# Fused attention and mixture-of-experts layer: how GpSimd issues its row scatters, k copies, bias and weight loads during attention

## What is computed

```python
x = L0_attn_hidden_states                       # 32 x 256 x 128, float32
xn = _layernorm(x)
# layer: pre-norm attention with factored weights, 16 heads of 8, causal, then a gelu MLP with factored weights
Q = einsum(LN(xn), q_U, q_V) + q_b              # K and V alike
attn = softmax(where(causal, Q K^T / sqrt(8), -1e9));  ctx = attn V
h = xn + ctx @ out_U @ out_V + out_b
layer = h + gelu(LN(h) @ fc1_U @ fc1_V + fc1_b) @ fc2_U @ fc2_V + fc2_b
# experts: softmax over 9, the best 2 of each token, silu-gated feed-forward of width 352
out = sum over the 2 chosen e of cw[t, e] * ((silu(xn Wg[e]) * (xn Wu[e])) @ Wd[e])
return x + layer + out
```

## Time and profile before

| | us |
|---|---|
| median of 3 runs | 1068.63 (1065.06 to 1071.98) |
| the profiled execution | 1073.31 |
| its span, first to last instruction | 1071.6 |
| TensorE busy | 997.1 (93%) |
| VectorE busy | 709.6 (66%) |
| ScalarE busy | 559.6 (52%) |
| GpSimd busy | 432.5 (40%) |

### The profile page before, as it was taken

One profiled execution on the slowest core, in us unless ns is written; L12 is line 12 of the kernel. 1 busy time (PEld: TensorE's weight loads), 2 busy tenths in 40 slices (PEclk: granted clock), 3 DMA queues, 4 the chain that ended last, 5 costly groups with the idle time before them and its releaser, 6 DMA issues. The chain is left out here.

```text
span 1071.6 us, 25659 instructions
## 1 busy us (share of the span) xinstructions
PE 997.1 (93%) x7829; PEld 773.1 (72%) x7829; DVE 709.6 (66%) x3240; ACT 559.6 (52%) x1285; POOL 432.5 (40%) x559
## 2 busy tenths in 40 slices
PE   4768999999999999999998895999999999899997
PEld 4535566666666666666655554999999999899996
DVE  5658589777777777777765661555555555457887
ACT  1552355556556556556553473555555555554442
POOL 9462032044544354444345442544544444441010
PEclk9675799999999999999999986999999999999999
DMA  8285276364464464454435213222222222218884
GB/s 228 81 228 170 78 206 180 82 165 120 102 153 112 122 160 121 101 114 109 109 93 113 84 58 103 64 67 61 64 62 64 72 64 60 81 40 254 236 236 129
DMA packets 133560, 127.16 MB, mean 119 GB/s; under 512 B 17274, under 2 KB 113652, under 8 KB 133428
## 3 DMA queue, kind: packets, MB, share of 16 engines
q1 hardware_dynamic: 109860, 67.83, 23.9%
q0 software_dynamic: 20592, 56.43, 19.5%
q10 hardware_dynamic: 2976, 1.26, 0.5%
HBM read 57.15 MB, written 42.60 MB: 93 GB/s over the span
## 5 line engine op out<-in xcount | busy, mean ns | idle before, releaser
L1363 DVE CUSTOM_DVE_ANT_0 att_masked_st<-att_m_ps,att_mask_st 128x128 bf16<-128x128 f32 (+1 forms) x1024 | 312.8, 353 | 122.2 <-PE att_m_ps L969 69.5
L784 ACT ACTIVATE att_probs<-att_t_ps 128x512 f32<-128x512 f32 x384 | 228.9, 598 | 219.6 <-PE att_t_ps L993 203.8
L625 POOL DMA_INDIRECT slot_x<-att_xs,att_slot_now x128 | 128.5, 1004 | 181.0 <-PE att_t_ps L993 130.9
L1616 POOL DMA_INDIRECT y_scratch<-moe_y,moe_row_now x136 | 132.8, 976 | 155.4 <-DVE moe_y L1870 102.8
L1864 DVE TENSOR_TENSOR moe_hidden<-moe_gate,moe_up_ps 128x352 f32<-128x352 f32 x136 | 70.9, 521 | 111.9 <-issue 85.3
L993 PE MATMUL att_t_ps<-att_mask_ts,att_ident_b 128*128 128x256 bf16 (+1 forms) x384 | 126.2, 329 | 0.0
L1693 PE MATMUL moe_y_ps<-w_down,moe_hidden_t 128*128 (+1 forms) x816 | 114.2, 276 | 3.8 <-DVE moe_y L1870 3.8
L1791 ACT ACTIVATE moe_gate<-moe_gate_ps 128x352 f32<-128x352 f32 x136 | 63.1, 464 | 96.8 <-PE moe_up_ps L1676 96.8
L1693 PEld LDWEIGHTS moe_y_ps<-w_down,moe_hidden_t 128*128 128x128 f32 (+1 forms) x816 | 101.8, 191 | 5.7 <-issue 5.5
L589 POOL DMA_DIRECT2D att_k_stack<-att_qk_parts x96 | 54.7, 575 | 89.3 <-PE att_t_ps L993 70.5
L992 PE MATMUL att_t_ps<-even_stack,att_k_stack 97*128 97x512 f32 x192 | 82.6, 430 | 4.1 <-DMA even_stack<-att_neg_max 3.8
(11 more groups left out here) (263 smaller groups left out, 2150.4 us busy)
## 6 DMA issues: line engine op xcount, KB each, us to landing
att_k_stack<-att_qk_parts POOLq DMA_DIRECT2D x96, 128.0 KB
slot_x<-att_xs POOLq DMA_DIRECT2D x17, 516.0 KB, 3.7
moe_x<-slot_x SPq DMA_DIRECT2D x34, 258.0 KB
att_xs<-xn_scratch SPq DMA_DIRECT2D x32, 256.0 KB
mlp_rows<-y_scratch POOLq DMA_DIRECT2D x16, 512.0 KB, 5.4
even_stack<-att_qk_parts SPq DMA_DIRECT2D x192, 32.0 KB
att_odd_stack<-att_qk_parts SPq DMA_DIRECT2D x192, 32.0 KB
xn_scratch<-att_probs POOLq DMA_DIRECT2D x16, 256.0 KB, 3.1
```

The source lines that it names most:

```text
L625: pool.indirect_dma_start(env["slot_x"][:], bass.IndirectOffsetOnAxis(ap=slot_now[c.parity][:, col:col + 1], axis=0), xs[c.parity][:, t, k ...
L784: act.activation(probs[:, m % PT, :], t_ps[m % 2][:], ACT.Exp).then_inc(exp_done, 1)
L1363: last = dve.tensor_tensor_reduce(out=masked_st[m % 2][:, part], in0=m_ps[m % 2][:, part], in1=mask_st[:, SEQ - width:], scale=1.0, scalar ...
L1616: pool.indirect_dma_start(env["y_dram"][:], bass.IndirectOffsetOnAxis(ap=row_now[q.parity][:, t:t + 1], axis=0), y[c.parity][:], None).the ...
```

## The change

GpSimd's step no longer goes by slots but by pairs of score units, 12 in a step. At every pair it waits for the first unit of the pair, and then issues at most one scatter or fill, at most one k part, the bias or one weight load.

- Scatters: 9 per step in steps 3 to 10, 12 per step in steps 11 to 14, and 8 in step 15, counted through over chunks (`ROWS_OF`, `ROWS_AT`).
- Fills: at the first 8 pairs of steps 0 and 1, and the first of step 2.
- k parts: one at each of the pairs 1, 2, 3 for (next chunk, b = 1), and at the pairs 8, 9, 10 for (chunk two ahead, b = 0).
- Bias at pair 7. Weight loads at the pairs 10 and 11 of steps 3 to 10.
- SyncE takes the chunk whose xs it loads from a table `XS_AT` made from the scatters' places, at one of three points of its step: a new one after the first 12 copies of q parts, after `stack_max(p, 1)`, and after `stack_max(next, 0)`.

```diff
-        LATE, PAIRED_FROM = 3, chunks - 3
-        XS_MID = {s: s - LATE + 1 for s in range(LATE - 1, PAIRED_FROM)} | {s: 2 * s - chunks + 1 for s in range(PAIRED_FROM, chunks)}
-        XS_LAST = {s: 2 * s - chunks + 2 for s in range(PAIRED_FROM, chunks - 1)}
+        LATE = 3
+        W_STEPS, LAST_ROWS = 8, 8
+        ROWS_OF = {step: 9 if step < LATE + W_STEPS else 12 for step in range(LATE, chunks - 1)} | {chunks - 1: LAST_ROWS}
+        ROWS_AT = {step: sum(n for k, n in ROWS_OF.items() if k < step) for step in ROWS_OF}
...
+        XS_AT = {(LATE - 1, 1): 0, (LATE - 1, 2): 1}
+        for c in range(2, chunks):
+            step, row = when(2 * TPC * (c - 1) - 1)
+            turn = (2 * row + 5) // 8
+            XS_AT[step + turn // 3, turn % 3] = c
...
-        def scatter_at(step, slot):
-
-            if LATE <= step < PAIRED_FROM and slot % 3 == 0:
-                return step - LATE, slot // 3
-            if step >= PAIRED_FROM and slot % 3 < 2:
-                k = slot // 3 * 2 + slot % 3
-                return 2 * step - chunks + k // (2 * TPC), k % (2 * TPC)
+        def scatter_at(step, pair):
+
+            if pair < ROWS_OF.get(step, 0):
+                j = ROWS_AT[step] + pair
+                return j // (2 * TPC), j % (2 * TPC)
             return None
...
+        def fill_at(step, pair):
+
+            if pair < 2 * TPC and step < LATE:
+                k = 2 * TPC * step + pair
                 return k if k < FILLS else None
...
+        def weights_at(step, pair):
+
+            if pair >= UNITS - 2 and LATE <= step < LATE + W_STEPS:
+                k = 2 * (step - LATE) + pair - (UNITS - 2)
                 return k if k < W_LOADS else None
             return None
+
+        K_SECOND_AT, K_FIRST_AT, BIAS_AT = (1, 2, 3), (8, 9, 10), 7
...
+                    if (p.index, 0) in XS_AT:
+                        load_xs(at(0, XS_AT[p.index, 0]))
...
-                    first, last = p.index == 0, p.index == last_chunk
-                    two_ahead = p.index < last_chunk - 1
-                    if not last:
-                        if not first:
-
-                            pool.wait_ge(scores_done, 2 * UNITS * p.index)
-                            pool.sem_inc(k_stack_free, 1)
-                        stack_k(at(half, d + 1), 1)
-
-                    add_bias(p)
-                    for slot in range(2 * UNITS):
-                        rows, blank_part, weights = scatter_at(p.index, slot), fill_at(p.index, slot), weights_at(p.index, slot)
-                        if p.index == LATE and slot == 0:
+                    x = p.index
+                    last = x == last_chunk
+                    two_ahead = x < last_chunk - 1
+                    for pair in range(HALVES):
+                        after_scores(p, 2 * pair + 1)
+                        rows, blank_part, weights = scatter_at(x, pair), fill_at(x, pair), weights_at(x, pair)
+                        if x == LATE and pair == 0:
                             pool.wait_ge(slots_ready, 1)
                             pool.wait_ge(zero_filled, 16 * FILLS)
                             pool.wait_ge(routed_all, 1)
-                        if rows is not None and rows[1] == 0:
-                            number_rows(at(0, rows[0]))
-                        if slot > 0 and (rows, blank_part, weights) != (None, None, None):
-                            after_scores(p, slot)
                         if rows is not None:
+                            if rows[1] == 0:
+                                number_rows(at(0, rows[0]))
                             scatter(at(0, rows[0]), rows[1])
                         if blank_part is not None:
                             fill(blank_part)
+                        if pair == BIAS_AT:
+                            add_bias(p)
+                        if pair in K_SECOND_AT and not last:
+                            stack_k_part(at(half, d + 1), 1, K_SECOND_AT.index(pair))
+                        if pair in K_FIRST_AT and two_ahead:
+                            if pair == K_FIRST_AT[0]:
+                                pool.wait_ge(k_split, x + 3)
+                                pool.sem_inc(k_stack_started, 1)
+                            stack_k_part(at(half, d + 2), 0, K_FIRST_AT.index(pair))
                         if weights is not None:
                             load_weights(weights)
-                        if slot == UNITS // TPC * STACK_AT and two_ahead:
-                            after_scores(p, slot)
-                            stack_k(at(half, d + 2), 0)
```

More of the change, by code:

```diff
@@ L317, in first_and_attention @@
         q_split, k_split, v_ready = s.sem("q_split"), s.sem("k_split"), s.sem("v_ready")
-        stack_free, k_stack_free, k_stack_started = s.sem("stack_free"), s.sem("k_stack_free"), s.sem("k_stack_started")
+        stack_free, k_stack_started = s.sem("stack_free"), s.sem("k_stack_started")
         q_stacked, k_stacked = ([s.two_sems(f"{n}_stacked_seq{b}_") for b in range(2)] for n in "qk")
@@ L344, in first_and_attention, with when @@
+        assert sum(ROWS_OF.values()) == chunks * 2 * TPC
+        def when(j):
+            step = max(k for k, n in ROWS_AT.items() if n <= j)
+            return step, j - ROWS_AT[step]
+        XS_AT = {(LATE - 1, 1): 0, (LATE - 1, 2): 1}
[3 more added lines that the diff above has]
+            XS_AT[step + turn // 3, turn % 3] = c
+        assert len(XS_AT) == chunks
         W_GROUP, W_PARTS = 3, 2 + len(FF_CHUNKS)
@@ L345, in first_and_attention @@
         W_LOADS = EXPERTS // W_GROUP * W_PARTS
-        def scatter_at(step, slot):
-            if LATE <= step < PAIRED_FROM and slot % 3 == 0:
-                return step - LATE, slot // 3
-            if step >= PAIRED_FROM and slot % 3 < 2:
-                k = slot // 3 * 2 + slot % 3
-                return 2 * step - chunks + k // (2 * TPC), k % (2 * TPC)
-            return None
-        def fill_at(step, slot):
-            if slot % 3 == 1 and step < 3:
-                k = 2 * TPC * step + slot // 3
+        def scatter_at(step, pair):
+            if pair < ROWS_OF.get(step, 0):
+                j = ROWS_AT[step] + pair
+                return j // (2 * TPC), j % (2 * TPC)
+            return None
@@ L360, in fill_at @@
+        def fill_at(step, pair):
+            if pair < 2 * TPC and step < LATE:
+                k = 2 * TPC * step + pair
                 return k if k < FILLS else None
             return None
-        def weights_at(step, slot):
-            if slot % 6 == 5 and slot < 12 and step >= LATE:
-                k = 2 * (step - LATE) + slot // 6
+        def weights_at(step, pair):
+            if pair >= UNITS - 2 and LATE <= step < LATE + W_STEPS:
+                k = 2 * (step - LATE) + pair - (UNITS - 2)
@@ L374, in first_and_attention @@
         HALVES = 2 * UNITS // 2
-        STACK_AT = 5
-        assert UNITS // TPC * STACK_AT >= UNITS
         Q_AT, K_AT, V_AT = (1, 5), (2, 6), 4
@@ L487, in step @@
                         sp.wait_ge(zero_filled, 16 * FILLS)
-                    if p.index in XS_MID:
-                        load_xs(at(0, XS_MID[p.index]))
+                    if (p.index, 1) in XS_AT:
+                        load_xs(at(0, XS_AT[p.index, 1]))
                     if two_ahead:
@@ L496, in step @@
                         stack_max(at(half, d + 1), 0)
-                    if p.index in XS_LAST:
-                        load_xs(at(0, XS_LAST[p.index]))
+                    if (p.index, 2) in XS_AT:
+                        load_xs(at(0, XS_AT[p.index, 2]))
                 stacks = first_stacks()
@@ L581, in load_weights, with stack_k_part @@
                                        w["Wd"][some, at_row:at_row + rows, :].rearrange("e p d -> p e d")).then_inc(experts_loaded, 16)
+                def stack_k_part(c, b, part):
+                    cols = slice(b * SEQ, (b + 1) * SEQ)
+                    pool.dma_start(k_stack[c.parity][32 * part:32 * part + 32, :, cols].bitcast(F32),
+                                   (k_hi, k_lo, k_hi)[part][:, cols].bitcast(F32)).then_inc(k_stacked[b][c.parity], 16)
                 def stack_k(c, b):
@@ L586, in stack_k @@
                     pool.sem_inc(k_stack_started, 1)
[L587 to L590, removed]
+                    for part in range(PARTS):
+                        stack_k_part(c, b, part)
                 pool.wait_ge(ln_ready, 1)
```

## The result

The changed kernel takes 1056.43 us (median of 4 runs, 1054.06 to 1058.80), the kernel before 1067.13 beside it: a ratio of 0.9893, 95% interval [0.9851, 0.9936], 10.7 us less. The forecast was 1051.0, its range 1044 to 1067. The time lies in the range, 5.4 us above the forecast.

What follows compares the result with a forecast made beforehand. TensorE (93% busy) was taken to bind, held up by GpSimd's scatter bursts. 1073.3 - 14.5 - 4.0 - 2.3 + 2.2 + 1.0 = 1055.7 us, less 4.7 for the median: 1051.0; range 1044 to 1067.

Steps and rivals of the forecast that it cites:

- Bursts stop the engines, and not rate or number: Steps 13 and 14: close scatters hold up VectorE and ScalarE, half clock follows; spacing them removes 14.5 us; chance 0.72.
- rivals 1 and 2: Stops from mean scatter rate: 1079.6 us, chance 0.10; or 0.9 us per scatter beyond 8: 1065.5 us, chance 0.07.
- rival 3: Stops come with the last three steps, not from their scatters: about 1070 us, no change; chance 0.06.
- -14.5: Steps 13 and 14: with 12 spaced scatters instead of 16, their whole excess goes, -14.5 us; bounds 0 and -14.5.
- -4.0: Step 15: 8 scatters instead of 16 save 3.4 us of lost clock and 0.6 us of stop; bounds 0 and -4.0.
- The bound of 0 for step 15: Step 15 may gain nothing: without maximum units for the next chunk it may fall to the lower clock by itself.
- Two of the signs: No two scatters closer than 2 us in steps 3 to 14; TensorE's clock 1.00 from step 1 to mid step 15.
- The row of maxima: Step ends: the row waits one 0.16 us packet in each of 14 steps, +2.2 us; bounds 0 and +16.8.
- Rival 4: Bursts gone, but the late row of maxima costs 1.2 us at each of 14 boundaries: 1065.6 us; chance 0.05.
- End of the stage: The last burst's stop makes ScalarE's context copy 2.32 us late on the ending chain; removing it gives -2.3 us.
- Fills: Steps 0 and 1: 8 fills in 15 slots instead of 24, +0.5 us each; bounds 0 and another 1.2 each.
- xs, k parts, bias: Steps of attention: moved xs loads, k parts and bias cost 0, the added waits hidden or followed only by GpSimd's work.

Runs made afterwards that it cites:

- high occasion: The first comparison and the fourth group of runs, in which the kernel before, unaltered, took 1065 to 1072 us.
- late_spaced: Kernel after, with the 8 scatters of step 15 one per pair at pairs 4 to 11, behind the pair's second unit: 1055.33 us.
- late_burst: Kernel after, with the 8 scatters of step 15 all in a row at pair 8: 1057.11 us.
- burst6_again: Kernel after, with the 12 scatters of steps 11 to 14 issued six at a time, at pairs 0 and 6: 1094.00 us.
- low occasion: The second and third groups of runs, in which the kernel before, unaltered, took 1045 to 1061 us (medians 1050.66 and 1052.45).
- burst3: Kernel after, with the scatters of steps 11 to 14 issued three at a time, at pairs 0, 3, 6 and 9: 1052.66 us.
- scatter_only: Kernel before with after's table of scatters and of xs; k parts, bias, fills and weight loads in their old slots: 1045.60 us, ratio to before 0.9938.
- before_third: Kernel before, unchanged, run again in the fourth group: 1072.23 us.
- before_again: Kernel before, unchanged, run once more with a profile: 1052.26 us, ratio to before 0.9998.
- after_again: Kernel after, unchanged, run again: 1057.62 us, ratio to the kernel before 1.0049.
- w_off_row: Kernel after, with only the weight loads of steps 3 to 10 moved to pairs 0 and 6: 1044.89 us, ratio to the kernel before 0.9944.
- before_w_late: Kernel before, with only the weight loads of steps 3 to 10 moved to slots 21 and 23, beside the row: 1063.57 us, ratio to before 1.0131.

## Why the prediction was right and where it was not

**Bursts stop the engines, and not rate or number: right, under a condition that I had not seen.** At 12 scatters per step on the high occasion, spaced ones (after, late_spaced, late_burst) take 129.0 to 129.7 us for steps 11 to 14 and bursts of six take 175.3. This is the same number and the same rate, so rivals 1 and 2 are refuted, and rival 3 with them, as stops now came in steps 11 and 12, where none had been. burst6_again is one execution, but its stops stand in the trace at seven of eight bursts. But the same bursts cost nothing on the low occasion (128.3). A burst is needed, and something else besides. The two low groups ran on two different chips and the fourth group on the same chip as the third, so it is not the chip alone. What it is stays open, and how a burst stops the other engines is not shown either: the release of nearly every stop is "remote".

**Steps 13 to 15: -19.6 against -18.5.** The terms -14.5 and -4.0 came out at -15.7 and -3.9. That is the bound of each term and slightly more, since step 14 without stops is not an ordinary step: it takes 30.3 to 30.5 in every run without stops but burst3 (31.4). I had measured the excess against 32.3. Step 15 without half clock takes 25.1 to 25.3. The bound of 0 for step 15, falling to the lower clock by itself, did not come up here, but scatter_only had such a stretch with no stop ahead of it (6.8 us at half clock, the step 28.0 us), so that the 3.9 need not all be due to the stops.

Two of the signs that I had named for this did not come. In after, eight scatters of steps 3 to 14 are issued less than 2 us behind the one before, as little as 1.38; but never more than two stand so close, and no stop follows. And TensorE's clock is not at 1.00 all the way, for the reason that follows.

**The row of maxima: +2.2 forecast, +9.8 measured in steps 3 to 10.** This is the step that failed: the term was mis-sized. The price of one packet, 0.16 us, was the wrong unit. At the three ends at which a 528 KB load is issued just ahead of the row, the time from the row's issue to the score is 1.5 to 1.6 us longer (3.87, 4.07, 3.79 against 2.27, 2.47, 2.25), 4.7 us in all. The other five ends have 1.3 together. And behind the long waits stands what I had priced nowhere: half clock, 3.4 us of it twice, 1.7 lost each. 4.7 + 1.3 + 3.4 = 9.4 of the 9.8. In the eight traces with the loads beside the row seven have one or two such stretches in steps 3 to 10, behind one of these waits; the six traces without have none there. My upper bound, 16.8 in all, held, but its price of 1.2 per end was too low at three ends and too high at the others. Rival 4 is what happened, at three ends instead of 14; I gave it 0.05. The note against it ("in step 1 the queues are far fuller") misled: a full queue says little, a large transfer just ahead of the row says much.

The prediction says that the trace of before has no such meeting. It has two, at the ends of steps 0 and 1, where a fill of 516 KB is issued 0.74 us ahead of the row. The first, from the timelines of GpSimd, SyncE and TensorE:

```profile
141.94 0.53 POOL L565 DMA_DIRECT2D slot_x<-att_xs  x1 [3.29 <-PE att_t_ps L993]
...
142.68 0.55 SPq L457 DMA_DIRECT2D att_odd_stack<-att_neg_max  x1
...
146.12 0.50 PE L992 MATMUL att_t_ps<-att_odd_stack,att_k_stack 97*128 97x512 f32 x1 [1.02 <-DMA att_odd_stack<-att_neg_max]
```

From the row's issue to the score it is 3.44 us here and 3.15 at the second, against 2.27 at the ends of steps 3 and 4. These two would have given a price of 0.9 to 1.2 us for one large transfer, more than five times mine. (After moves the fills away, and has 2.28 and 2.27 there.)

"DMA: Bandwidth & Descriptors" of the Trainium skill, section "Queues, rings and completion order", spoke against the change, and it was right. The number that I drew from it was not: I took its packet for one packet of the profile's count, 0.16 us, while the page's packet is typically 9 to 17 descriptors. What the row met stands in the packet records of the trace of after, at the end of step 3. The load is 128 records of 4224 bytes, 8 for each of the 16 engines, each share closed by a record of 4 bytes; the first ones take up to 0.96 us, most later ones 0.16. The row is 16 records of 1024 bytes, one for each engine. In the kernel before they start 1.2 to 1.4 us after the row's issue, here 2.2 to 2.6, and every one of the 16 starts within 6 ns behind a closing record. So by these times (the trace does not name the engines) the row waited on each engine until the load's whole share was through, and not for one record of it. The trace agrees with the page if a record is one descriptor: a share is then 9 of them. At the end of step 6, where the load is issued 0.26 us ahead of the row, the row's records start while part of the load is still to come.

**End of the stage: -2.3 forecast, -5.9 measured, by another mechanism.** I read ScalarE's stop of 2.32 us at 650.11 as lying on the chain that ends the stage. It does not. Three times, from the last score unit, the last scatter's issue and the last store of h to the first load of the next block (SyncE's and GpSimd's timelines; us):

```
                      from score   from scatter   from store of h
before        (high)     14.89         10.55            3.75
before_third  (high)     14.89         10.56            3.74
before_again  (low)      14.87         10.54            8.08
after         (high)      8.97         16.56            2.18
after_again   (low)       8.95         16.54            2.17
w_off_row     (low)       8.96         16.55            2.17
late_spaced   (high)     10.73          9.23            2.47
late_burst    (high)     14.87          9.25            2.28
```

In the unaltered kernel before, the time from the last scatter is constant to 0.02 us, stop or no stop; in after and w_off_row the time from the store of h is. So before, GpSimd's work ended the block, and the chain of h had 1.6 us to spare even with the stop (3.75 - 2.17). After, GpSimd is through in time and h ends the block. The first rows of the end on SyncE, of before and of after:

```profile
656.37 0.36 SPq L463 DMA_DIRECT2D h_scratch<-att_h  x1
660.12 0.92 SPq L1562 DMA_DIRECT2D moe_x<-slot_x  x2
```

```profile
643.97 0.36 SPq L474 DMA_DIRECT2D h_scratch<-att_h  x1
646.15 0.92 SPq L1576 DMA_DIRECT2D moe_x<-slot_x  x2
```

What fills the 10.55 us is not the scatter's way to HBM. By the packet records the last of its data starts 1.7 us after the issue, and GpSimd, which waits for all scatters to land, is past that wait within 2.4 us. Behind it stands GpSimd's closing instruction of the block, a DRAIN, at the line of the block itself. Of before, of before_w_late and of after:

```profile
L391 POOLq DRAIN  x1: 7749/7749/7749, 652.1 to 652.1; - x1
L391 POOLq DRAIN  x1: 7014/7014/7014, 645.9 to 645.9; - x1
L402 POOLq DRAIN  x1: 6442/6442/6442, 637.4 to 637.4; - x1
```

It begins 2.55 us after the last scatter's issue in before, takes 7.75 us and ends 0.25 us ahead of the first load: 10.55. In before_w_late it takes 7.01, and the load comes 9.82 us after the last scatter. In after GpSimd has issued its last scatter at 629.6 and waits only for one of the last score units; its DRAIN runs from 637.4 to 643.8, under the chain of h. Over all the runs it takes 6.4 to 7.8 us; what sets its length is open.

The gain is therefore the same on both occasions. scatter_only has it too (9.0 us from the last score unit to the load in its trace), and takes 6.9 us less than the kernel before beside it, in a low group where no stop was to be won. late_spaced and late_burst put the last scatter back to 636.6. In both GpSimd's DRAIN begins at 639.15, takes 6.44 us, and the load comes 9.2 us behind the scatter, whether it was spaced or at the end of a burst of 8; the store of h is 2.47 and 2.28 ahead, slightly over its own 2.17. So neither a backlog in a burst nor the length of a scatter decides, as I had expected of one or the other, but when GpSimd gets to the end of its program.

**Fills: +1.0 forecast.** Steps 0 to 2 took 2.6 more in the first comparison. Step 0 varies between 46.4 and 50.8 with programs alike there, so its part can't be told. Steps 1 and 2 have -1.1 and +1.2, no cost that shows. **xs, k parts, bias: 0,** right: GpSimd has no wait for xs of over 1 us, and moving a k part off the row changed nothing measurable.

**The sum.** 1073.3 - 19.6 - 5.9 + 9.8 + 2.6 + 0.5 - 1.4 - 0.7 = 1058.6, against 1058.8 for the profiled execution. Against the forecast, steps 13 to 15 and the stage's end gave 4.7 more, and the row of maxima took 7.6 more. The medians lie 5.4 us from the forecast and the profiled executions 3.1, because that of after is only 2.4 over its median where I had carried over 4.7. That these two errors partly cancel is luck: the 3.6 us more at the end came by a mechanism that I had not seen. The forecast of faster by over 1% held by a hair (1.07%) and for the reason that it gave, on the high occasion. That the first comparison fell on one is luck too. On the low one the reason is absent. What is left there in the traces of after_again and before_again is -5.9 at the end, +7.8 in steps 3 to 10 (265.8 against 258.0) and +1.1 in steps 11 to 14, 3.0 us in all, and the change is 0.5% slower (5.2 us by the medians). The two traces also differ where the change has no part that can be told: after_again is 3.5 us shorter in steps 0 to 2 and 3.3 longer in the block behind. w_off_row, which keeps the change and moves two loads per step, has the gain at the end (9.0 us) and not the cost: 0.9944 on the low occasion; on the high one it was not run.

## What to carry to other kernels

Before a transfer is moved, find the small transfers with no slack whose landing ends a wait, and issue no large load just ahead of one: here that cost 1.6 us each, ten times one packet record, and sometimes half clock stood behind it. Price such a meeting from one that the trace already has, as at the ends of steps 0 and 1 here. Let GpSimd finish its part of a block some 8 us ahead of the other engines, as its DRAIN took up to 7.8. Tell which of two chains ends the block by which of the two distances stays constant over several runs, and then look at every instruction of that chain, those that count as no busy time too. Run the kernel before again in each group, since a gain that rests on a condition of the chip shows only while the condition is there.

## What the runs showed of the hardware that was not expected

- The same program, with bursts of indirect DMAs issued by GpSimd 1.27 us apart, took 1052.14 us on one occasion and 1094.00 on another. On the second, ScalarE or VectorE stopped for 2.9 to 4.4 us in seven of eight bursts of six, with 61.4 us at half clock behind. Scatters one per pair of units (about 2.7 us apart, two of them at times 1.4) brought no stop on either occasion.
- GpSimd's DRAIN at the end of a block took 7.75 us in all three executions of the kernel before, 7.01 in before_w_late and 6.44 in after, late_spaced and late_burst. Where the last indirect DMA was late, it began 2.5 to 2.6 us behind that DMA's issue, and the new block waited for it. From a store by SyncE to the new block it was 2.17 us.
- A 16 KB row on SyncE's queue, 2.25 us from issue to use alone, took 3.6 to 5.1 us with a 528 KB load from GpSimd's queue issued just ahead, and 2.25 with one issued 0.58 us behind it (before_w_late, step 8). At the end of step 3 of after each of the row's 16 packet records started within 6 ns behind a record that closes a share of the load.
- A wait of TensorE of 1.4 us could be enough for 3.4 us at half clock (after 248.68 and 415.85), and one of 1.66 (at 349.89) had none behind it. In after_again, the same program, only the shortest of the three (1.26, at 409.38) had one.
